# Two gated cross-attention blocks on one core: first transfers reordered, late loads moved into the attention, raws a step sooner, two rows' query low parts by GpSimd

## The reference

```
x = x + tanh(g_xattn[0]) * L0_xattn(layernorm(x), ctx, ctx, ...)
# L0_xattn
Q, K, V = heads(queries @ Wq.T + bq), heads(keys @ Wk.T + bk), heads(values @ Wv.T + bv)   # 16 heads of 16
scores = einsum('bhqd,bhkd->bhqk', Q, K) / sqrt(16)
attn = softmax(scores - 0.1 * |t_key - t_query|)
out  = einsum('bhqk,bhkd->bhqd', attn, V) ... @ Wo.T + bo
```

## Time and profile before

| | us |
|---|---|
| median of 3 runs | 740.12 (739.31 to 741.78) |
| the profiled execution | 741.31, of it span 739.5 |
| busy in the span | PE 691.2, DVE 567.0, ACT 453.1, POOL 368.8 |
| first scores of the first layer | at 72.85 |
| mean granted clock of PE | 0.991 |

### The profile page before, as it was taken

How to read it: one execution, slowest core, us unless ns; L and a number is a source line. 1 busy time by engine, 2 the same in 40 slices (tenths; PEclk the granted TensorE clock), 3 DMA queues, 4 the chain that set the end, 5 groups by cost and what they waited for, 6 DMA issues and landing times.

```text
span 739.5 us, 12829 instructions
## 1 busy us (share of the span) xinstructions
PE 691.2 (93%) x4390; PEld 434.9 (59%) x4390; DVE 567.0 (77%) x1037; ACT 453.1 (61%) x972; POOL 368.8 (50%) x442
## 2 busy tenths in 40 slices
PE   7886999999999899999999999999999899999993
PEld 5654444444443588788663444444444688999983
DVE  6786899999993267575888999999997667666673
ACT  3413888888888464856316888888887324333330
POOL 4641566565555433864500022645662756665543
PEclk9998999999999999999999999999999999999998
DMA  5898645555545434003134455432201432211100
GB/s 184 273 252 220 204 148 178 185 152 181 178 168 217 137 97 132 26 1 101 43 104 121 124 156 180 130 97 78 78 2 60 120 127 73 66 38 44 34 9 16
DMA packets 51423, 87.56 MB, mean 118 GB/s; under 512 B 8661, under 2 KB 16855, under 8 KB 51360
## 3 DMA queue, kind: packets, MB, share of 16 engines
q1 hardware_dynamic: 43184, 71.39, 31.1%
q0 software_dynamic: 4640, 11.54, 5.6%
q10 hardware_dynamic: 3536, 3.81, 2.0%
HBM read 44.92 MB, written 41.63 MB: 117 GB/s over the span
## 4 chain that ended last, share of the span: by engine, by line
PE 59%; POOL 10%; issue 9%; DVE 8%; SPq 5%; DMA 5%; ACT 2%; POOLq 0%; another core or an unknown queue 0%; DVEq 0%; ACTq 0%
PE ps_out L856 10%; PE ps_wide L1053 6%; PE ps_out L1076 6%; PE ps_wide L725 6%; PE ps_a L839 6%; SPq L517 3%; PE ps_a L978 3%; PE ps_misc L839 3%; POOL w_lo L1377 3%; PE ps_a L635 2%; PE ps_a L1065 2%; DMA stack_q<-planes_q 2%; PE ps_out L992 2%; PE ps_wide L652 2%; PE ps_misc L992 1%
## 5 line engine op out<-in xcount | busy, mean ns | idle before, releaser
L1688 DVE TENSOR_REDUCE row_max<-ps_wide 128x2 f32<-128x1024 f32 x256 | 301.7, 1220 | 21.1 <-PE ps_wide L725 20.3
L1199 ACT ACTIVATE probs<-ps_a 128x512 f32<-128x512 f32 (+1 forms) x418 | 199.1, 522 | 28.6 <-PE ps_a L839 26.7
L725 PE MATMUL ps_wide<-stack_k,stack_q 48*128 48x512 f32 x512 | 145.1, 470 | 11.6 <-DVE row_max L1688 4.3
L839 PE MATMUL ps_a<-stack_q,stack_k 62*128 62x512 f32 (+3 forms) x418 | 137.3, 391 | 2.1 <-ACT probs L1199 1.5
L856 PE MATMUL ps_out<-probs,vals 128*17 128x512 f32 x1024 | 134.1, 598 | 0.5 <-POOL probs L1455 0.5
L1199 ACT ACTIVATE probs<-ps_misc 128x512 f32<-128x512 f32 (+1 forms) x222 | 114.0, 514 | 16.5 <-PE ps_misc L839 13.8
L1455 POOL TENSOR_TENSOR probs<-probs,fixes_sb 128x512 f32<-128x512 f32 x64 | 82.2, 1284 | 79.1 <-ACT probs L1199 79.1
L839 PEld LDWEIGHTS ps_a<-stack_q,stack_k 62*128 62x128 f32 (+1 forms) x418 | 63.5, 184 | 67.4 <-ACT probs L1199 30.9
L725 PEld LDWEIGHTS ps_wide<-stack_k,stack_q 48*128 48x128 f32 x512 | 68.4, 184 | 47.0 <-DVE row_max L1688 26.2
L839 PE MATMUL ps_misc<-stack_q,stack_k 62*128 62x512 f32 (+3 forms) x222 | 87.8, 396 | 1.3 <-ACT probs L1199 1.2
L839 PEld LDWEIGHTS ps_misc<-stack_q,stack_k 62*128 62x128 f32 (+1 forms) x222 | 40.9, 184 | 39.1 <-ACT probs L1199 30.4
(11 more groups left out here) (288 smaller groups left out, 1413.1 us busy)
## 6 DMA issues: line engine op xcount, KB each, us to landing
rows_sorted<-blank SPq DMA_DIRECT2D x17, 1040.0 KB, 5.0
planes_k<-planes SPq DMA_DIRECT2D x32, 256.0 KB, 3.7
planes_q<-planes SPq DMA_DIRECT2D x32, 256.0 KB, 3.8
stack_k<-planes_k SPq DMA_DIRECT2D x64, 128.0 KB, 2.9
stack_q<-planes_q SPq DMA_DIRECT2D x64, 128.0 KB, 2.8
w_raw<-in_L_W SPq DMA_DIRECT2D x6, 1024.0 KB, 5.3
stack_k<-planes_k SPq DMA_DIRECT2D x64, 64.0 KB, 2.6
stack_q<-planes_q SPq DMA_DIRECT2D x64, 64.0 KB, 2.7
```

The costliest lines, as they stand in the source:

```text
L725: mm(raw_slot(l, ("pair", g, p))[:, i * S:(i + 1) * S], stack_q[at, slot(g, c) + q * P:slot(g, c) + (q + 1) * P], stack_k[at, slot(g, c):s ...
L839: mm(score_slot(("tile", n))[:, start:end], stack_k[at, slot(g, c) + k * P:slot(g, c) + (k + 1) * P], stack_q[at, slot(g, c) + start:slot( ...
L1199: do(probs[n % PROBS[l]][:, j, start:end], score_slot(("tile", n * TILES + t))[:, start:end], ACT.Exp, scale=0.25).then_inc(exp_done, 1)
L1688: v.tensor_reduce(row_max[:, g % 2, :, p], raw_slot(l, ("pair", g, p))[:].rearrange("p (i k) -> p i k", i=2), AX, ALU.max).then_inc(sem(f" ...
```

## The change

1. SP's first nine transfers are in another order, and w_k, the context, w_v, x and w_q have a semaphore each; identity and the three small biases share one. w_v's high part is now written by ACT, before by DVE.
2. In `load_rest` three transfers are left (gates, fixes, bias_o). w_o, bias_2, b1 and order are issued by SP behind the second layer's weights.
3. POOL broadcasts the constant rows over the first half of the ring only. SP copies that half to the second, behind the last stack of the prologue. Group 2 is the first that waits for it.
4. `FIRST_RAWS` begins at the values of row 2, before at the q projection of row 2. SP loads each of the first stacks whole, before in two parts with stores between.
5. For rows 2 and 3 (`b >= LATE`) ACT writes the full value of q too, and POOL subtracts (`planes_low`). PE then waits for ACT's high part instead of the low one.

```diff
+LATE = 2
-FIRST_RAWS = {(2, "q", 0): (0, 2), (2, "q", 1): (2, 2),
-              (3, "k", 0): (4, 2), (3, "k", 1): (6, 1), (3, "v", 0): (7, 1), (3, "v", 1): (8, 2),
+FIRST_RAWS = {(2, "v", 0): (0, 1), (2, "v", 1): (1, 1), (2, "q", 0): (2, 2), (2, "q", 1): (4, 2),
+              (3, "k", 0): (6, 1), (3, "k", 1): (7, 1), (3, "v", 0): (8, 1), (3, "v", 1): (9, 1),
               (3, "q", 0): (10, 2), (3, "q", 1): (12, 2)}
...
 # SP
                     store_planes("k", 0)
                     store_planes("q", 0)
-                    planes_left(sp, 0, C)
-                    load_stacks(0, "k")
+                    planes_left(sp, 0, 2 * C)
+                    load_stacks(0)
                     store_planes("k", 1)
-                    planes_left(sp, 0, 2 * C)
-                    load_stacks(0, "q")
                     store_planes("q", 1)
-                    load_stacks(1, "k")
+                    load_stacks(1)
                     store_planes("k", 2)
-                    load_stacks(1, "q")
                     store_planes("q", 2)
...
                     load_stacks(RING - 1)
+                    sp.wait_ge(sem("rows_in0"), 16 * 2 * N_ATT)
+                    sp.wait_ge(loaded_rest, 16 * (N_FIRST + N_REST))
+                    for i in range(2):
+                        for rows in constant_rows(i):
+                            sp.dma_start(rows[:, RING * S:].bitcast(F32), rows[:, 0:RING * S].bitcast(F32)).then_inc(loaded_rest, 16)
...
                     for s_ in "kvq":
-                        sp.dma_start(w_qkv[s_][:], part(a[f"L1_W{s_}"])).then_inc(sem("w_layer1"), 16)
+                        sp.dma_start(w_qkv[s_][:], part(a[f"L1_W{s_}"])).then_inc(loaded_context, 16)
+                    for dst, src in ((w_o[:], part(a["L0_Wo"])), (bias_2[:], a["L0_b2"].partition_broadcast(P)),
+                                     (b1_cols[:], a["L0_b1"]), (order[:], a["order"])):
+                        sp.dma_start(dst, src).then_inc(loaded_context, 16)
...
 # PE
-            pe.wait_ge(loaded_keys, 16 * N_KEYS)
...
-                pe.wait_ge(*made(0, "q", "planes_ready", B - 1, c))
+                pe.wait_ge(*made(0, "q", "proj_high", B - 1, c))
             attention(0)
...
 # ACT, unit_out
-                if not query:
-                    if b > 0:
+                if not query or (l == 0 and b >= LATE):
+                    if query:
+                        act.wait_ge(*made(l, "k", "planes_ready", b, c))
+                    elif l == 0 and b > LATE:
+                        act.wait_ge(*made(l, "q", "planes_ready", b - 1, c))
+                    elif b > 0:
                         act.wait_ge(*made(l, "k", "planes_ready", b - 1, c))
                     do(full[:, c, :], ps[c][:], **how)
...
 # ACT, start
-            act.wait_ge(loaded_keys, 16 * N_KEYS)
-            load_inputs(1)
+            act.wait_ge(loaded_context, 16)
             for c in range(C):
                 do(ctx_hi[:, c, 0:S], context_of(0)[:, c, :], ACT.Copy).then_inc(sem("parts_high"), 1)
+            act.wait_ge(loaded_values, 16)
+            do(w_v_hi0[:], w_qkv["v"][:], ACT.Copy).then_inc(sem("parts_high"), 1)
+            load_inputs(1)
+            act.wait_ge(loaded_rest, 16 * N_FIRST)
...
 # POOL
                     for i in range(2):
                         for rows, n in zip(constant_rows(i), (NB, MP + NB)):
-                            pool.dma_start(rows[:, S:].rearrange("r (n t) -> r n t", t=S),
-                                           rows[:, 0:S].unsqueeze(1).broadcast_to([n, RING * 2 - 1, S])).then_inc(sem("rows_in0"), 16)
-            split_maximum(0, 0)
+                            pool.dma_start(rows[:, S:RING * S].rearrange("r (n t) -> r n t", t=S),
+                                           rows[:, 0:S].unsqueeze(1).broadcast_to([n, RING - 1, S])).then_inc(sem("rows_in0"), 16)
+                if b == B - 1:
+                    split_maximum(0, 0)
+                if b >= LATE:
+                    planes_low(0, "q", b)
```

95 lines of the change are left out of this document (50 added, 45 removed).

## The result

| | before | after |
|---|---|---|
| median (us) | 740.32 (739.31 to 741.78, 4 runs) | 751.24 (751.03 to 751.45, 4 runs) |
| ratio, 95% interval | | 1.0142 [1.0123, 1.0161] |
| the profiled execution, its span | 741.31, 739.5 | 751.31, 749.5 |
| mean granted clock of PE | 0.991 | 0.98 |

The changed kernel is 1.4% slower, outside the range of 735.5 to 745.0. The forecast was 741.0.

What follows compares the result with a forecast made beforehand. The bound was taken as shared, the SyncE queue and what clogs it. Group 1's start (-1.4 us) and the clock (+2.3) summed to +0.9, giving a median of 741.0 us, range 735.5 to 745.0.

Steps and rivals of the forecast that it cites:

- the start of the first scores: End of the prologue: scores start at 65.9 instead of 72.85, 6.95 us won.
- First loads: Prologue start: first projection at 6.95 instead of 8.02; row 1's k projection at 20.2 instead of 21.92, 1.7 us won.
- Where it worked before: First loads: VectorE's w_q_lo, behind ScalarE waiting for the last small load, was taken to run about when it did before.
- Stack 0 and the stores of k1: Rows 1 to 2: eight loads precede k1's stores, which land in 4.0 us; row 2's q projection at 41.35, before 41.19.
- Row 2's q low parts on GpSimd: Row 3's root waits behind two low parts of 1.25 us each: ready at 51.3, before 49.2; normal rows end at 53.5.
- The raws: Rows 2 and 3: raws 2 to 5 finish before the root; PE idles about 2.8 us at raw 8; scores start at 65.9.
- What is late next: Group 1: PE waits 5.7 us for SyncE's maximum send; eight added transfers cost 4.4; group 1 starts at 82.45, -1.4 us.
- The clock: Behind group 1's stall: half-speed work for up to 6.6 us loses 0 to 3.3 us; 2.3 taken.
- rival 3: Prologue: added idle before raw 8 drops the clock there too, last q output after about 66.3; 743.5 up to 746; 25%.
- The sum: Whole kernel: -1.4 + 2.3 = +0.9 us, span 739.5 becomes 740.4.

Runs made afterwards that it cites:

- e2: Changed kernel with the first nine transfers, their waits and w_v's high part as in the kernel before; 749.83 us, ratio 1.012.
- e10: Changed kernel with row 3's inputs issued by ScalarE behind row 1's k outputs, not its q outputs; 747.14 us, ratio 1.009.
- e4: Changed kernel with all query low parts on VectorE again and PE waiting for them before the attention; 748.21 us, ratio 1.0103.
- e7: e6 with the raws a step sooner, as in the changed kernel; 744.21 us, ratio 1.0027 to the kernel before.
- e6: Kernel before with GpSimd's broadcast halved and four late loads moved to SyncE; copies, late loads and weights spread over groups 0 to 2; 740.99 us, ratio 0.9997.
- e1: Changed kernel with the four copies, three weights and four late loads issued behind the send of group 1's maximum; 750.2 us, ratio 1.0121.
- e5: Changed kernel with the eleven transfers (copies, weights, late loads) spread over groups and each clearing one group later; 742.89 us, ratio 1.0033.
- e8: e6 without the spreading: copies and late loads stand in front of the send of group 1's maximum; 745.82 us, ratio 1.0063.
- e17: Kernel before with only the halved broadcast and its four copies behind the first send, weights ahead of that send; 736.99 us, ratio 0.9963.
- e14: Kernel before with the halved broadcast, four copies behind the first send, and layer 1's weights issued in groups 1 and 2; 737.66 us, ratio 0.9946.

## Why the prediction was wrong

The step that failed is the start of the first scores: the forecast had the prologue 6.95 us shorter, at 65.9, and it was 2.0 us longer, at 74.89. Four of its terms failed on the way there, the first loads, the landing of k row 1's stores, VectorE beside GpSimd, and the raws. The wait behind it was forecast in kind, and came 2.1 us longer than forecast.

**First loads: failed.** The projection did start at 7.08 as forecast (6.95). But k of row 1 came at 23.51, not 20.2 and later than before's 21.92. "Where it worked before" was the wrong phrase: bias_v is now the ninth and last of the first transfers, and ScalarE's first k output waited for it until 11.29, before 9.68. ScalarE's weight cast, VectorE's w_q_lo and the value additions queue behind that, PE idles 3.12 us at 16.08, and q0 then runs at 1.2 GHz (1.22 us for two, 0.64 at 23.51). I had noted this chain and priced it at nothing. e2, with the old order, has 21.73 at this place, and the other kernels with the new order 21.93 to 22.73. So no profile has the 1.7 us that I put as won, and this profile is the latest of them.

**Stack 0 and the stores of k1: right in order, short in size.** The loads start 3.6 us later than forecast (30.39 against 26.8), 3.3 of them carried on from the start. (In e2 the stores of q0 went out 2.0 us sooner and these loads only 0.7, so the start's lateness is partly hidden here.) The landing took 7.3 us instead of 4.0, another 3.3. So the k output came at 43.74, not 37.1. I took a landing time from a row whose stores had no company and did not ask what ScalarE issues at 35 us. e10 moved only those inputs and got 3.7. (The eight loads are 0.68 us each by the rows and not 0.66, which changes little.)

**Row 2's q low parts on GpSimd: mechanism right, one cost missing.** The root came behind them, at 56.41 to 57.45 instead of 51.3, mostly for the lateness before it. (For the end of the normal rows behind it the forecast's own terms give 53.2, not its 53.5.) Missing was that VectorE is slower beside GpSimd: newton took 1.25 and 1.20 us for what takes 0.15 and 0.17 in the kernel before and 0.16 and 0.16 in e10, where GpSimd was idle then. That is 2.1 us ahead of the raws. e4, without GpSimd's part, has S 4.6 sooner and a time 3.0 less, the latter within the intervals.

**The raws: failed as a gain.** PE's idle time ahead of raw 8 was 3.52 us, forecast 2.8. With a stack that is late the sooner raws move PE's wait ahead of the projection (1.42 at 41.04; 3.57 in e7, where S came 3.85 us later than in e6). No run shows a gain from them; that they cost time is shown by S in one profile and not by e7's interval.

**What is late next: right in kind, too small.** The wait for `stack_q<-max_rows` was the largest single loss, as forecast: 7.82 instead of 5.7. The queue in front of it grew by 6.2 instead of 4.4, since a copy took 0.72 to 0.89 where I put 0.62 and a weight 1.20 where I put half a microsecond. With S at 65.9 it would have been a loss of 0.3 against before, as group 1 stands at S + 18.28: 84.2. e1, e5 and e8 confirm the mechanism and add the correction that a send further back is hit just as well.

**The clock: right.** Half-speed work behind the wait lost 1.6 us, from 9.33 at group 1 to 10.93 at the end of the attention; 2.3 was forecast, 0 to 3.3 the bounds. Not in the sum were three slow stretches of the prologue, at 18.64, at 47.32 and from 64 to 67. The last stands behind the 3.52 us of waiting at raw 8, as rival 3 had it.

**The sum** was -1.4 + 2.3 = 0.9. The terms were +9.33 + 1.6 - 0.9 (given back after the attention) = +10.0. Of the 10.7 us between -1.4 and 9.33 the start of the scores has 9.0 and the send 1.7. From S to the end of the attention the forecast had 185.7 us (250.74 + 0.9 - 65.9), and 186.78 was measured. So the attention was foreseen to about 1 us, and the miss against the forecast is the prologue. The loss against the kernel before is another sum: of its 10.9 us at that place the attention has 8.9 (186.78 - 177.89), of which e5 gives back 7.8 by spreading the eleven transfers, and S has 2.0. S moves by up to 3 us between executions, but the changed prologue had 73.98 at the least. Rival 3 named a late prologue and a lower clock in it, decided by a last q output later than 66.3; it was at 73.16. Its price of 5 us at most left out that the delays add up: each of the steps had a bound of its own, and the range was not made from all of them failing the same way. One thing I had not separated at all was the part that was good: halving GpSimd's broadcasts. It is worth 0.4% with its four copies behind the first send (e17), 0.5% with the weights spread too (e14), and was hidden under the rest.

## What to carry to other kernels

An issuing queue that is busy for three quarters of each period has a budget: count the transfers per period, and spread what is added, each in a period in which nobody waits for it; the place in front of or behind one urgent transfer matters less. Take a transfer's landing time from a row with the same company, and list what every other queue issues in those microseconds. When several things change at once, make each alone: here the one good part was worth 0.4%, and the kernel with all of them was 1.4% slower.
